# Moving two row sums per head pair from GpSimd to VectorE, and a bias from VectorE to GpSimd

## The reference, cut to what matters

```python
energy = jnp.einsum('bhqd,bhkd->bhqk', q, k)
att = jax.nn.softmax(energy, axis=-1) / D ** 0.5
out = jnp.einsum('bhqk,bhkd->bhqd', att, v)
out = out @ Wp.T + bp
h1 = out + hidden
```

## Time and profile before

| | us |
|---|---|
| median of 3 runs (2829.6 to 2831.0) | 2829.73 |
| the profiled execution: span from the first to the last instruction | 2834.1 |
| PE busy in the span | 2640.4 (93%) |
| DVE busy | 2166.8 (76%) |
| POOL busy | 1972.5 (70%) |
| ACT busy | 1825.0 (64%) |

### The profile page before, as it was taken

The page is one execution under the profiler, slowest core; times in us unless marked ns, Lnnn a source line. Parts: engine busy times, 40 slices in busy tenths (PEclk is TensorE's granted clock), DMA queues, the critical chain, the costliest instruction groups (busy, mean ns, idle before and its releaser), DMA issues. The chain is left out here.

```text
span 2834.1 us, 60784 instructions
## 1 busy us (share of the span) xinstructions
PE 2640.4 (93%) x21715; PEld 1468.0 (52%) x21761; DVE 2166.8 (76%) x4459; ACT 1825.0 (64%) x3298; POOL 1972.5 (70%) x1579
## 2 busy tenths in 40 slices
PE   7899999999999999999959998999899999977997
PEld 5655466554665547655425554555455445533443
DVE  5777678776787768877577778776877687748997
ACT  4366654665556655566456677667766776667886
POOL 0289724896249962599548997989789888975442
PEclk9999999999999999999979999999999999998999
DMA  6122443224432334323122313321432232245444
GB/s 231 39 58 58 135 130 117 58 58 146 123 101 58 77 126 143 93 58 102 64 78 58 80 43 105 80 58 31 116 80 58 54 94 58 62 176 160 100 100 108
DMA packets 168755, 260.30 MB, mean 92 GB/s; under 512 B 85388, under 2 KB 91668, under 8 KB 167576
## 3 DMA queue, kind: packets, MB, share of 16 engines
q1 hardware_dynamic: 166680, 250.27, 32.3%
q0 software_dynamic: 1792, 6.33, 0.6%
HBM read 99.15 MB, written 38.88 MB: 49 GB/s over the span
## 5 line engine op out<-in xcount | busy, mean ns | idle before, releaser
L502 DVE TENSOR_REDUCE a_mxs<-ps 128x1 f32<-128x512 f32 x2048 | 1268.8, 682 | 258.4 <-PE ps L371 256.0
L463 ACT ACTIVATE a_p<-ps 128x512 f32<-128x512 f32 x2048 | 1043.0, 605 | 202.0 <-PE ps L385 191.8
L342 POOL TENSOR_TENSOR a_sum<-a_p 128x512 f32<-128x512 f32 x768 | 986.1, 1293 | 126.6 <-PE ps L403 103.9
L371 PE MATMUL ps<-a_k,a_q 96*128 96x512 f32 x2048 | 857.0, 425 | 24.1 <-DVE a_mxs L502 20.5
L385 PE MATMUL ps<-a_q,a_k 98*128 98x512 f32 x2048 | 810.7, 419 | 18.5 <-ACT a_p L463 11.6
L347 POOL TENSOR_TENSOR a_sum<-a_sum,a_p 128x512 f32<-128x512 f32 x512 | 664.5, 1298 | 40.2
L403 PE MATMUL ps<-a_sum,a_unit 128*32 128x512 f32 x1536 | 659.9, 601 | 12.8 <-POOL a_sum L347 11.8
L403 PE MATMUL ps<-a_p,xv 128*32 128x512 f32 x3968 | 647.1, 600 | 1.6 <-DVE tok L521 1.6
L371 PEld LDWEIGHTS ps<-a_k,a_q 96*128 96x128 f32 x2048 | 389.9, 190 | 258.3 <-DVE a_mxs L502 105.1
L385 PEld LDWEIGHTS ps<-a_q,a_k 98*128 98x128 f32 x2048 | 384.1, 189 | 257.2 <-ACT a_p L463 161.9
L472 ACT ACTIVATE a_ots<-ps 128x512 f32<-128x512 f32 x256 | 152.8, 598 | 417.4 <-PE ps L403 416.4
(11 more groups left out here) (249 smaller groups left out, 2999.6 us busy)
## 6 DMA issues: line engine op xcount, KB each, us to landing
a_q<-qh SPq DMA_DIRECT2D x256, 128.0 KB, 2.3
a_k<-kh SPq DMA_DIRECT2D x256, 128.0 KB, 2.4
a_q<-ql SPq DMA_DIRECT2D x128, 128.0 KB, 2.3
a_k<-kl SPq DMA_DIRECT2D x128, 128.0 KB, 2.4
x<-a_p SPq DMA_DIRECT2D x64, 256.0 KB, 2.1
a_p<-in_w_fc SPq DMA_DIRECT2D x12, 1024.0 KB, 7.8
kh<-in_x SPq DMA_DIRECT2D x4, 2048.0 KB, 14.3
a_p<-x SPq DMA_DIRECT2D x16, 512.0 KB, 5.9
```

The costliest lines, as they stand in the source:

```text
L342: pair = pool.tensor_tensor(tile, self.key_tile(u, kt), self.key_tile(u, kt + 1), ALU.add)
L371: pe.matmul(self.mx[self.mx_ring[at]], self.q[j][0:96, t * P:(t + 1) * P], self.k[j][0:96, half * HALF:(half + 1) * HALF], start=True, sto ...
L463: act.activation(self.key_tile(u, kt), self.st[self.st_ring[CHUNKS * k + n]], ACT.Exp, scale=self.scale).then_inc(self.s_exp, 1)
L502: dve.reduce_max(self.mxs[:, k % 2, c:c + 1], self.mx[self.mx_ring[CHUNKS * k + c]], axis=AX.X).then_inc(self.s_mxr, 1)
```

## The change

Sums j = 2 and j = 8 go to VectorE. `run_dve` calls `sums_dve` at the end of every step; `DVE_EACH = ((2, 0, 4), (8, 1, 4))` puts sum 2 behind the reductions of step 4 of the even head, sum 8 behind those of step 4 of the odd head. `DVE_SUMS` is empty. VectorE has semaphores of its own for its sums, and the value rounds that read one wait for it. GpSimd skips both sums and keeps the other ten, 18 adds for a pair. In layer 0 the 8 bias adds go from `spare` to GpSimd's queue behind its sums; the waits for the two loads go with them. Before the attention of layer 0's first batch VectorE also waits for three stores that read the memory of the sum buffers.

```diff
+    DVE_EACH = ((2, 0, 4), (8, 1, 4))
+    DVE_SUMS = ()
...
+    def sum_tiles(self, eng, M, j):
+
+        u, r = j // self.PER_HALF % 2, j % self.PER_HALF
+        prior = self.SUM_PRIOR[j]
+        eng.wait_ge(self.s_pv, self.ROUNDS * (M - (prior > j)) + self.SUM_USED[prior] + 1 + self.PV_CREDIT)
+        return self.sum[:, self.SUM_AT[j], :], [self.key_tile(u, kt) for kt in range(3 * r, min(3 * r + 3, TT))]
...
     def sums(self, pool, N, M, j):
...
+        if self.by_dve(M, j):
+            return
...
+    def sums_dve(self, dve, M, k, s):
+
+        each = tuple((j, k - k % 2 + odd, step) for j, odd, step in self.DVE_EACH if k < H)
+        for j, head, step in each + self.DVE_SUMS if M % (H // 2) == H // 2 - 1 else each:
+            if (head, step) != (k, s):
+                continue
+            tile, keys = self.sum_tiles(dve, M, j)
+            dve.wait_ge(self.s_exp, self.exps_to(M, j, len(keys)))
+            pair = dve.tensor_tensor(tile, keys[0], keys[1], ALU.add)
...
+            else:
+                pair.then_inc(self.s_sum_dve, 1)
...
-        pe.wait_ge(self.s_sum, 2 * self.PER_HALF * E + used[-1] + 1)
+        pe.wait_ge(self.s_sum, self.pool_sums(E // 2, used[-1]))
+        if any(self.by_dve(E // 2, j) for j in used):
+            pe.wait_ge(self.s_sum_dve, self.dve_sums(E // 2, used[-1]))
...
                 if s == 2 and ok(k + 1):
                     self.m_parts(dve, N + 1, (k + 1) % NJ)
+                self.sums_dve(dve, H // 2 * b + min(k, H - 1) // 2, k, s)
...
                     pool.wait_ge(s_late, 48 * (b + 1))
+                    pool.wait_ge(s_res, 16 * (b + 1))
+                    for t in range(TT):
+                        pool.tensor_tensor(h1[:, t, :], h1[:, t, :], bp, ALU.add).then_inc(s_xb, 1)
...
-                        if i == 0:
-                            dve.wait_ge(s_res, 16 * (b + 1))
-                            dve.wait_ge(s_late, 48 * (b + 1))
-                            if not last:
-                                dve.wait_ge(s_x, 16 * (b + 2))
+                        if i == 0 and not last:
+                            dve.wait_ge(s_x, 16 * (b + 2))
                         if i < TT:
-                            dve.tensor_tensor(h1[:, i, :], h1[:, i, :], bp, ALU.add).then_inc(s_xb, 1)
...
+                    if b == 0:
+                        dve.wait_ge(s_gout[2], 16)
+                        dve.wait_ge(s_gout[3], 16)
+                        dve.wait_ge(s_gout[KC], 32)
                     att.run_dve(dve, b, spare)
```

More of the change, by code:

```diff
@@ L211, in __init__ @@
         self.s_part, self.s_sum = sem("part_sum"), sem("sum_ok")
+        self.s_part_dve, self.s_sum_dve = sem("part_sum_dve"), sem("sum_dve_ok")
+        self.pool_parts = self.dve_parts = 0
         self.s_ots = sem("ots_ok")
@@ L333, in key_tile, with by_dve @@
         return self.p[:, 4 * u + kt // 2, kt % 2 * HALF:(kt % 2 + 1) * HALF]
-    def sums(self, pool, N, M, j):
[L337 to L343, removed]
+    def by_dve(self, M, j):
+        return j in [n for n, _, _ in self.DVE_EACH] or M % (H // 2) == H // 2 - 1 and j in [n for n, _, _ in self.DVE_SUMS]
@@ new lines, in pool_sums, with dve_sums @@
+    def pool_sums(self, M, j):
+        return sum(not self.by_dve(m, i) for m in range(M) for i in range(4 * self.PER_HALF)) + sum(not self.by_dve(M, i) for i in range(j + 1))
+    def dve_sums(self, M, j):
+        return 4 * self.PER_HALF * M + j + 1 - self.pool_sums(M, j)
+    def sum_tiles(self, eng, M, j):
[3 more added lines that the diff above has]
+        return self.sum[:, self.SUM_AT[j], :], [self.key_tile(u, kt) for kt in range(3 * r, min(3 * r + 3, TT))]
@@ L344, in sums, with exps_to @@
+    def exps_to(self, M, j, n):
+        return CHUNKS * (2 * M + j // (2 * self.PER_HALF)) + TT * (j // self.PER_HALF % 2) + 3 * (j % self.PER_HALF) + n + self.EXP_CREDIT
+    def sums(self, pool, N, M, j):
+        if self.by_dve(M, j):
+            return
+        tile, keys = self.sum_tiles(pool, M, j)
+        pool.wait_ge(self.s_exp, self.exps_to(M, j, 2))
+        pair = pool.tensor_tensor(tile, keys[0], keys[1], ALU.add)
+        if len(keys) == 3:
             pair.then_inc(self.s_part, 1)
-            pool.wait_ge(self.s_part, 2 * (2 * N + u) + r + 1)
@@ L346, in sums @@
-            pool.wait_ge(self.s_exp, CHUNKS * N + TT * u + kt + 2 + 1 + self.EXP_CREDIT)
-            pool.tensor_tensor(tile, tile, self.key_tile(u, kt + 2), ALU.add).then_inc(self.s_sum, 1)
+            self.pool_parts += 1
+            pool.wait_ge(self.s_part, self.pool_parts)
+            pool.wait_ge(self.s_exp, self.exps_to(M, j, 3))
+            pool.tensor_tensor(tile, tile, keys[2], ALU.add).then_inc(self.s_sum, 1)
         else:
             pair.then_inc(self.s_sum, 1)
+    def sums_dve(self, dve, M, k, s):
[6 more added lines that the diff above has]
+            pair = dve.tensor_tensor(tile, keys[0], keys[1], ALU.add)
+            if len(keys) == 3:
+                pair.then_inc(self.s_part_dve, 1)
+                self.dve_parts += 1
+                dve.wait_ge(self.s_part_dve, self.dve_parts)
+                dve.tensor_tensor(tile, tile, keys[2], ALU.add).then_inc(self.s_sum_dve, 1)
+            else:
+                pair.then_inc(self.s_sum_dve, 1)
```

## The result

The changed kernel takes **2880.5 us** (median of 4 runs, 2874.8 to 2883.5) against 2829.7 (2829.6 to 2831.0): a ratio of 1.0175, 95% interval 1.016 to 1.0189. It is slower, by 51 us where the prediction said 54.

What follows compares the result with a forecast made beforehand. The prediction took TensorE (PE) to pace each pair of heads, with a hidden dependence on VectorE's fifth reduction. Terms +68 and -14 us gave +54 on 2829.7, so 2884 us; range 2866 to 2953.

Steps and rivals of the forecast that it cites:

- The slot on the fifth reduction: Each VectorE sum delays the burst's fifth reduction and so PE's eighth maximum matmul: 112 x 0.61 = +68 us.
- Twice the same interval behind the reduction: In both bursts the eighth maximum matmul starts 0.19 to 0.20 us behind the fifth reduction, so it already waits, without margin.
- some 0.2 us behind the fifth reduction as before: Sign of being right: the eighth maximum matmul keeps this interval, with PE idle before it.
- The even heads, no contest: GpSimd sits waiting for round 0 when VectorE's even-head sum starts, so its slot is 0.61 us.
- The odd heads, VectorE first by 0.06: VectorE's odd-head sum starts 0.06 us before GpSimd's sum 9 and takes the shared port: slot 0.61 us.
- the first rival: In odd heads GpSimd's sum 9 starts first, VectorE's slot is 1.8 us: 67 us more, 2951 us; chance 0.25, wholly or partly.
- The ends of the batches: In the last pairs PE's waits for GpSimd's sums and VectorE's divide go: -14 us, bounds -8 and -20.
- no PE wait for sums at the ends: Sign of being right: PE's 11.8 + 1.0 us of waits for GpSimd's sums at batch ends disappear.
- The bias on GpSimd: Layer 0's bias adds, 10.2 us behind GpSimd's last sum, finish before needed: nothing, at worst 1 us in three batches.
- the sums fit into VectorE's idle time: Rival: VectorE idles 5.8 us a pair, the sums need 1.2, so only batch ends count: 2816 us; chance 0.09.
- GpSimd is the pace: Rival: GpSimd's list sets the pair's time, so moving 128 adds saves 87 us: 2743 us; chance 0.02.

Runs made afterwards that it cites:

- half the slots: Changed kernel with only the odd heads' sum 8 on VectorE, the even heads' sum back on GpSimd: 2850.5 us, ratio 1.008.
- the two short instructions: Changed kernel with no sum on VectorE; two 16-column reductions behind the fourth reduction of every head instead: 2832.3 us, ratio 1.001.
- the delayed sums: Changed kernel with one 16-column reduction put ahead of each sum on VectorE: 2993.3 us, ratio 1.0581.
- the last kernel: Changed kernel with VectorE making three sums in each batch's last pair and none in other pairs: 2815.5 us, ratio 0.9954.
- the bias alone: Changed kernel with all twelve sums of a pair back on GpSimd, so only the bias adds move: 2825.4 us, ratio 0.9988.

## Why the prediction was right, point by point

**The slot on the fifth reduction,** +68 us by the prediction: it is 62.7. The mechanism is shown: one step later the loss is gone, with half the slots it is halved. The size was off by one reading: "Twice the same interval behind the reduction says that it waits for it already." It did not quite. The matmul stood 0.19 us behind the reduction by its order in the queue and now starts 0.06 behind it, and the prediction's "some 0.2 us behind the fifth reduction as before" was wrong. Of these 0.13 us most is lost again, because the matmul that has waited takes 0.50 us instead of 0.39 and the transposes follow it 0.43 later instead of 0.32. Net, 0.03 to 0.04 us a head were free: by the two short instructions 0.03, by the sums 0.60 - 0.56 = 0.04. 112 x 0.56 = 62.7.

**The even heads, no contest:** right, 0.68 us in all 56. **The odd heads, VectorE first by 0.06:** right in all 56, by 0.038 to 0.071; that nothing but this margin stood between the forecast and the first rival, the delayed sums show. The Trainium skill, "SBUF — State Buffer", section "SBUF: two separate sides", has whoever starts first keep the shared port for its whole instruction. The traces agree: 0.68 us with VectorE ahead by 0.04 us or more, 1.79 to 1.83 with GpSimd ahead by 0.04 us or less.

**The ends of the batches,** -14 us: -12 by the medians (51 against 62.7). In the profiles it is -15.1, but there before's span is 4.4 us above the median of its runs, as the prediction noted, and the changed kernel's only 1.2. The term is in part another than was said. The prediction took back all 14.4 us of waits for sums and the divide, and named "no PE wait for sums at the ends" as a sign; 4.4 us of them are left, so 10.0 came back. Another 1.6 us are a wait that it did not have, of the score matmuls for the loads of row maxima, before and after:

```profile
PE ps L385 <- DMA a_q<-a_mrow: 2.9, 4, 1.3
...
PE ps L429 <- DMA a_q<-a_mrow: 1.3, 1, 1.3
```

In the four kernels with pairs of 28.2 us or more it is 1.3, in the others 2.2 to 3.6: it goes with the length of the pairs, so it is no gain of having fewer sums on GpSimd. GpSimd's last sums can be shortened further by giving VectorE more of them just there, as the last kernel shows.

**The bias on GpSimd, at nothing:** right. GpSimd's timeline in layer 0's first batch:

```profile
348.70 9.88 POOL L903 TENSOR_TENSOR kh<-kh,qh 128x512 f32<-128x512 f32 x8
```

VectorE's first use of what these adds make:

```profile
361.97 0.68 DVE L1456 TENSOR_TENSOR kh<-ps,kh 128x512 f32<-128x512 f32 x1
```

They end at 358.58, 3.4 us ahead of it; in the fourth batch it is 1.5 us, and no piece is late in any.

**The rivals.** That the sums fit into VectorE's idle time was refuted for this place, and is true one step on: there the time is 2824.6 and the pair 27.67. That GpSimd is the pace is refuted by its wait of 4.76 us and by the kernel with the sums one step later, which gains nothing over the bias alone.

So the forecast's 54 us were 68 - 14 and are 63 - 12: two small misses of opposite sign, and that the sum came out within 3 us is in part luck.

## What to carry to other kernels

Before work is put into an engine's idle time, find out which instruction of that engine releases the bottleneck and put the work behind it: here one step in the list is worth 56 us at the same load on every engine. Freeing an engine that the bottleneck makes wait in every round gained nothing here; look for the places where the wait runs the other way, here the last pair of a batch. And a bottleneck whose row says busy throughout may still be waiting; delaying the suspected releaser by a small known amount measures its slack.

## What the runs showed of the hardware that was not expected

The shared port goes by order of start to within hundredths of a microsecond: with VectorE ahead by 0.038 to 0.071 us its add takes 0.68 us, with GpSimd ahead by 0.001 to 0.041 us 1.79 to 1.83, in 56 of 56 places each time. When GpSimd comes second, its own add is stretched from 1.28 us, the more the smaller VectorE's lead: to 1.63 us at 0.18 us, to 1.76 at 0.05.

A stall that left TensorE idle for 1.5 us was followed by a granted clock of 0.50 to 0.60 over the next 3 us in 20 of 56 pairs, which cost 1.5 us more each; in the other 36 the same stall left the clock at 1.00, and so did the stalls of 0.56 us in the changed kernel's pairs shown. What decides between the two is not shown. So a stall can cost its own length once more, and a sum of stalls that leaves the clock out comes out too low.
